# Moving work of a decoder's second layer from VectorE to ScalarE, TensorE and GpSimd

## The chip, the core and the metric

The program runs on one core of a Trainium2 chip. Five engines work beside each other and wait for one another only by semaphores: TensorE (PE, matrix products into PSUM), VectorE (DVE), ScalarE (ACT), GpSimd (POOL) and SyncE (SP, which issues transfers). The metric is the device time of one execution in microseconds (us).

## The reference

Two sequences of 512 rows by 128 columns pass through six sublayers, each followed by a layer norm of the sum with its input. The change lies in the second one (the program's "layer 2"), a cross attention with a state-space filter:

```python
Q = (x_text @ Wq).reshape(Bb, Tt, H, DH)              # Bb = 2, Tt = 512, H = 4
K = (x_vision @ Wk).reshape(Bb, Gg, H, DH)            # Gg = 77
scores = einsum('bthd,bghd->bhtg', Q, K) / sqrt(DH)   # masked by vision_mask
topv, topi = top_k(scores, 32)
attn = zeros_like(scores).at[..., topi].set(softmax(topv))
c_t = einsum('btg,bgd->btd', attn.mean(axis=1), x_vision @ Wv) * text_mask[..., None]
x = layernorm(x_text, g_norm_in, b_norm_in)
scale_in, shift_in = split(c_t @ W_film_in + b_film_in, 2)
x = x * (1.0 + mod_gate * scale_in) + mod_gate * shift_in
y = s4d(x, ...)                                       # two Fourier products and a filter
scale_out, shift_out = split(c_t @ W_film_out + b_film_out, 2)
xt = x_text + y * (1.0 + mod_gate * scale_out) + mod_gate * shift_out
h = layernorm(xt, g_ffn, b_ffn)
xt = xt + gelu(h @ W1 + b1) @ W2 + b2
return layernorm(xt, g_norm_out, b_norm_out)
```

## The kernel before, in words

The 1024 rows are eight tiles of 128 (`g` = 0 to 7), four to a sequence, which the code calls a half (`b` = 0, 1). Each engine runs a fixed list of steps, written out by hand in `first_layers`; a step is a small function, and a semaphore counts what it has done. Products land in eight PSUM banks that are handed out in a fixed order (`ring`): `claim` waits until the bank's last content was read out, `ready` and `taken` wait for it to be filled or read out.

In layer 2 each tile passes through these steps. TensorE makes its scores (`score`) and ScalarE copies them from PSUM (`scores`). VectorE takes the 32 largest of each row and head (`select`, four rounds of eight). GpSimd subtracts the maximum (`shift`), ScalarE takes the exponent (`exp`), GpSimd zeroes what was not selected (`weigh`), VectorE sums and inverts the sums and multiplies them by the text mask (`invert`), GpSimd multiplies and adds up the heads (`average`). For tiles 6 and 7 VectorE does the averages itself.

When the four averages of a half are there, TensorE turns them (`mean`), multiplies by the values (`c`, copied by ScalarE as `cT`) and by the film weights `xa_wfilm` (`film`, one product of 512 columns for each tile, in two alternating banks for half 0 and in four for half 1). VectorE reads each film bank out as film = gate * bank + `film_const`. `film_const` holds the gated bias, with 1 added to the scales, on all 128 rows; it is made early from a product of a row of ones with the bias row. For half 0 GpSimd then applies the film to `u`, the normalised input (`scale(0)`); for half 1 VectorE does. TensorE transforms `u` forth (`forth`), VectorE multiplies by the filter (`multiply`, `combine`), TensorE transforms back (`back`), VectorE adds up (`modulate`) and normalises (`norm_ff`), and the feed-forward part follows (`up`, gelu, `down`, `leave`, `move`, `finish`).

The input's normalisation is `norm_in`: VectorE takes moments, ScalarE a logarithm and an exponent for the root, VectorE refines it (`settle`) and scales four tiles (`Norm.scale`, L229). GpSimd then applies gain and bias (`affine`).

The order of the steps around the change is, on VectorE: select(2), invert(1), norm_in(0), select(3), invert(2), norm_in(1), invert(3), select(4), film(0), select(5), invert(4), select(6), invert(5), multiply(0), combine(0), select(7). On GpSimd, after weigh(3): affine(0), average(3), shift(4), weigh(4), the move of the output bias, scale(0), shift(5), average(4), skip(0), weigh(5). On TensorE: kernel, score(5), mean(0), film(0), score(6), score(7), forth(0), back(0), mean(1), film(1), up(0), size, forth(1), down(0), back(1).

Of the kernel before, what the change touches and what calls it, by code (L numbers as in the profile page):

```python
# [202 lines left out]
class Norm:  # L203
# [3 lines left out]
    def __init__(self, core):  # L207
# [11 lines left out]
        self.on_dve = self.on_act = self.shifts = self.to_apply = 0  # L219
# [16 lines left out]
    def shifts_of(self, dve, step, src, eps=1e-5):  # L236

        self.refine(dve, step, src, eps)
        k = (self.on_dve - 1) % 2
        if self.shifts:  # L240
            dve.wait_ge(self.applied, HT * self.shifts)
# [4 lines left out]
    def apply(self, act, src, dst):  # L246

        k = (self.on_act - 1) % 2
        self.to_apply += 1
        act.wait_ge(self.shift_ready, self.to_apply)  # L250
        for i in range(HT):
            act.activation(dst[:, i], src[:, i], ACT.Identity, scale=self.root[:, k, i:i + 1],  # L252
                           bias=self.shift[:, i:i + 1]).then_inc(self.applied, 1)
# [174 lines left out]
def linear_attention(core, sb, kernel, x, out):  # L428
# [36 lines left out]
    def order():  # L465
        out = [("features", 0), ("score", 0), ("features", 1)]
        for g in range(NT):
# [7 lines left out]
                   "consts": ["keys", "values", "consts"]}  # L475
# [260 lines left out]
K_TOP = 32  # L736

# [231 lines left out]
def cross_attention_ssm(core, x, x_ready, early_ring, sums_read, out):  # L969
# [27 lines left out]
    film_const = sb("xa_film_const", [P, 2, 2, P])  # L997
# [21 lines left out]
    ring.update({name: early_ring[name] for name in ("keys", "values", "consts")})  # L1019
# [13 lines left out]
    w1_ready = sem("w1_ready")  # L1033
# [19 lines left out]
    def tensor(pe):  # L1053
        def consts():
# [11 lines left out]
            pe.wait_ge(ones_ready, 1)  # L1066
            s = ring["consts"]
            s.claim(pe)
            pe.matmul(s.ps[:, :], ones[:, :], t["film_bias"][:, :], start=True, stop=True).then_inc(s.filled, 1)
# [61 lines left out]
        def film_of(b):  # L1131
# [38 lines left out]
        def up_of(b):  # L1170
# [7 lines left out]
            if b == 0:  # L1178
                pe.wait_ge(w1_ready, 1)
# [21 lines left out]
    def scalar(act, step):  # L1201
# [42 lines left out]
        def columns_of():  # L1244
            move("norm_cols", norm_cols[:, :], lambda s: s.ps[:, 0:2])
            ring["norm_cols"].taken(act)
            act.mul(w1[:, :], t["xa_w1"][:, :], norm_cols[:, 0:1]).then_inc(w1_ready, 1)
# [8 lines left out]
        def round_experts():  # L1256
# [5 lines left out]
            for n in range(4):  # L1262
# [3 lines left out]
                "taps": taps, "columns": columns_of, "kernel": kernel_of, "round": round_experts,  # L1266
                "leave": lambda b: core.norm.apply(act, xt[:, half(b)], xt[:, half(b)]),
                "finish": lambda b: core.norm.apply(act, xt[:, half(b)], out[:, half(b)])}

    def gpsimd(pool, step):  # L1270
# [67 lines left out]
    def vector(dve, step):  # L1338
        def norm_in(b):

            dve.wait_ge(x_ready, HT * (b + 1))
            core.norm.dve(dve, step, x[:, half(b)], u[:, half(b)], ready=unit_ready)
# [20 lines left out]
        def invert(g):  # L1363
# [5 lines left out]
            step(dve.tensor_reduce(total[:, k], prob[:, k], AX.X, ALU.add))  # L1369
            step(dve.reciprocal(total[:, k], total[:, k]))  # L1370
# [98 lines left out]
        def finish(b):  # L1469
            core.norm.shifts_of(dve, step, xt[:, half(b)])  # L1470
# [5 lines left out]
        def setup():  # L1476
# [3 lines left out]
            for b in range(B):  # L1480
# [9 lines left out]
            s = ring["consts"]  # L1490
            s.ready(dve)
            const = s.ps[:, :].rearrange("p (o k c) -> p o k c", o=2, k=2)
            step.mark(dve.tensor_scalar(film_const[:, :, 0], const[:, :, 0], rows["mod_gate"], 1.0, ALU.mult,
                                        ALU.add))
            dve.tensor_scalar(film_const[:, :, 1], const[:, :, 1], rows["mod_gate"], None, ALU.mult
                              ).then_inc(s.drained, 1)
            s.taken(dve)
# [2507 lines left out]
```

## Time and profile before

| | |
|---|---|
| three runs | 590.97, 595.43, 594.78 us; median 594.78 |
| profiled execution, first to last instruction | 594.2 us, mean granted TensorE clock 0.880 |
| what lies around that span | 0.58 us, if the profiled execution is taken as one at the median |
| PE busy | 478.3 us (80%) |
| DVE busy | 431.7 us (73%) |
| ACT busy | 273.4 us (46%) |
| POOL busy | 248.9 us (42%) |

The shares are means over six sublayers with different limits, so they say little of one stage. The second layer runs from about 84 to 201 us of the span.

### The profile page before, as it was taken

How to read it: one execution, taken by the hardware profiler on the slowest of the kernel's cores; microseconds unless marked ns; L12 is line 12 of the kernel's file. 1: busy time of each engine (PE TensorE's matmuls, PEld its weight loads, DVE VectorE, ACT ScalarE, POOL GpSimd, SP SyncE). 2: the span in 40 equal slices, each digit the busy share in tenths (PEclk: the TensorE clock that was granted, in tenths of full speed). 3: DMA queues.
4: the chain of work that ended last, by engine and by line, in shares of the span. 5: the costliest groups of instructions: out<-in, count | busy, mean ns of one | idle time of the engine just before them, and what ended most of it. 6: DMA issues, size and time to landing. Idle time of an engine off the chain costs nothing. (4 is left out here: it accounts for less than half of the span.)

```text
span 594.2 us, 11914 instructions
## 1 busy us (share of the span) xinstructions
PE 478.3 (80%) x4082; PEld 361.4 (61%) x4082; DVE 431.7 (73%) x1456; ACT 273.4 (46%) x681; POOL 248.9 (42%) x295
## 2 busy tenths in 40 slices
PE   3888782779679685799898999887779879779994
PEld 1455442555648664777694668765358755369983
DVE  4687968797986846855687999996487748327743
ACT  4599570221213245355412768552335413547741
POOL 3631399456812102455201524340485333616650
PEclk9986895587789877799999999979878989969997
DMA  8300004410000005605200000000471500151113
GB/s 253 109 2 1 1 2 144 122 57 2 1 1 1 1 1 141 142 2 105 40 1 1 2 2 2 1 2 3 165 318 30 121 0 26 52 151 47 46 48 104
DMA packets 27998, 33.37 MB, mean 56 GB/s; under 512 B 4962, under 2 KB 21074, under 8 KB 27427
## 3 DMA queue, kind: packets, MB, share of 16 engines
q1 hardware_dynamic: 26002, 29.13, 16.8%
q0 software_dynamic: 1504, 3.15, 1.6%
q8 instruction: 34, 0.56, 0.4%
q10 hardware_dynamic: 432, 0.33, 0.2%
q14 instruction: 26, 0.21, 0.1%
HBM read 26.44 MB, written 6.16 MB: 55 GB/s over the span
## 5 line engine op out<-in xcount | busy, mean ns | idle before, releaser
L2133 POOL TENSOR_TENSOR ea_scaled_rows<-ea_scaled_rows 128x768 f32<-128x768 f32 (+2 forms) x21 | 24.0, 1142 | 50.7 <-ACT ea_scaled_rows L2047 49.6
L3725 POOL DMA_INDIRECT em_results<-em_y_slot,slot_rows x31 | 29.7, 958 | 28.7 <-DVE em_y_slot L3852 28.1
L288 ACT ACTIVATE norm_log<-norm_var 128x4 f32<-128x4 f32 x20 | 4.1, 205 | 73.6 <-DVE norm_var L269 73.6
L3584 PE MATMUL banks<-em_slotT,em_weights 128*128 128x128 f32 x248 | 35.0, 287 | 2.6 <-ACT em_weights L3473 2.6
L3843 DVE SCALAR_TENSOR_TENSOR em_innerT<-banks,em_bias_of,em_soft 128x128 f32<-128x128 f32 x62 | 18.9, 347 | 23.0 <-ACT em_soft L3667 20.2
L38 PE MATMUL banks<-ea_w_high,ea_x_high 128*128 128x384 f32 x64 | 27.2, 425 | 8.7 <-DVE ea_acc L2224 8.5
L3584 PEld LDWEIGHTS banks<-em_slotT,em_weights 128*128 128x128 f32 x248 | 32.1, 202 | 3.3 <-issue 3.3
L2047 ACT ACTIVATE ea_scaled_rows<-banks,ea_gate 128x192 f32<-128x192 f32 x64 | 23.3, 418 | 18.8 <-PE banks L38 18.6
L2795 POOL TENSOR_TENSOR ga_to_end<-ga_cum 128x512 f32<-128x512 f32 x8 | 9.1, 1137 | 45.0 <-DVE ga_to_mid L2857 45.0
L3667 ACT ACTIVATE em_soft<-banks,em_bias_of 128x128 f32<-128x128 f32 x62 | 19.4, 364 | 12.3 <-PE banks L3584 11.7
L38 PE MATMUL banks<-ea_w_high,ea_x_low 128*128 128x384 f32 x64 | 23.7, 371 | 0.0
L38 PE MATMUL banks<-ea_w_low,ea_x_high 128*128 128x384 f32 x64 | 23.7, 370 | 0.0
L3241 POOL TENSOR_TENSOR ca_prob<-ca_prob,ca_most 128x1232 f32<-128x1232 f32 x8 | 18.0, 2250 | 11.1 <-DVE ca_most L3293 11.1
L648 POOL TENSOR_TENSOR lin_q_strip<-lin_qT,lin_strip_head 128x512 f32<-128x512 f32 x8 | 9.5, 1199 | 29.6 <-PE banks L538 20.3
L3720 POOL DMA_INDIRECT em_slots<-em_sent,em_where x16 | 15.7, 981 | 14.2 <-DVE em_where L3794 9.6
L2220 DVE SCALAR_TENSOR_TENSOR ea_acc<-banks,ea_gate,ea_acc 128x192 f32<-128x192 f32 x24 | 10.0, 418 | 15.8 <-PE banks L38 15.5
L38 PEld LDWEIGHTS banks<-ea_w_high,ea_x_high 128*128 128x128 f32 x64 | 13.7, 214 | 11.0 <-DVE ea_acc L2224 9.6
L1356 DVE MATCH_REPLACE8 xa_left<-xa_top,xa_left 128x77 f32<-128x77 f32 x96 | 20.3, 225 | 0.0
L3596 PE MATMUL banks<-em_down,em_innerT 128*128 x124 | 18.9, 276 | 0.6 <-DVE em_innerT L3843 0.6
L538 PE MATMUL banks<-lin_q_strip,lin_kT 32*128 32x512 f32 x64 | 12.1, 832 | 8.8 <-DVE lin_scores L682 8.3
L3183 ACT ACTIVATE ca_prob<-ca_prob 128x1232 f32<-128x1232 f32 x8 | 9.8, 1231 | 19.7 <-POOL ca_prob L3241 19.7
L682 DVE TENSOR_TENSOR lin_scores<-banks,causal 128x2048 f32<-128x2048 f32 x8 | 18.2, 2272 | 0.0
(522 smaller groups left out, 1539.4 us busy)
## 6 DMA issues: line engine op xcount, KB each, us to landing
em_up<-in_em_up SPq DMA_DIRECT2D x3, 1536.0 KB, 10.8
ea_wide<-ea_gates SPq DMA_DIRECT2D x4, 1024.0 KB, 11.7
em_down<-in_em_down SPq DMA_DIRECT2D x3, 768.0 KB, 12.2
em_slots<-slot_rows SPq DMA_DIRECT2D x1, 2108.0 KB, 10.8
w_qkv<-in_w_qkv SPq DMA_DIRECT2D x1, 1536.0 KB, 7.4
slot_rows<-em_slots SPq DMA_DIRECT2D x1, 1360.0 KB, 8.5
cos_half<-in_cos_half SPq DMA_DIRECT2D x1, 1024.0 KB, 7.1
sin_half<-in_sin_half SPq DMA_DIRECT2D x1, 1024.0 KB, 9.3
```

The source lines that it names most:

```text
L38: ins = pe.matmul(out, weights[w], data[d], start=(start and n == 0), stop=(stop and n == 2), **kw)
L682: dve.tensor_tensor(scores[:, g % 2].rearrange("p r j t -> p (r j) t"), scored.rearrange("p r j t -> p (r j) t"), spread(causal[:, :], 1, ...
L1356: ins = dve.match_replace(left[:, k, hh], top[:, k, r, hh], src[:, k, hh], SELECTED)
L2047: ins = act.activation(scaled_rows[:, g % 2, j - 1 + n], s.ps[:, n * QKV:(n + 1) * QKV], ACT.Copy, scale=gate[:, g, e:e + 1])
L2133: step(pool.tensor_tensor(scaled_rows[:, k, 0:n], scaled_rows[:, k, 0:n], scaled_rows[:, k, n:2 * n], ALU.add))
L3241: pool.tensor_tensor(p, p, spread(most[:, g % AHEAD], 2, [P, H, G]), ALU.subtract).then_inc(shifted, 1)
L3584: ins = pe.matmul(s.ps[:, k * P:(k + 1) * P], weights[:, n % NW, k // 2, k % 2 * P:(k % 2 + 1) * P], slotT[:, n], start=True, stop=True, s ...
L3596: ins = pe.matmul(s.ps[:, 0:P], innerT[:, n % NW, j], down_all[:, bass.ds(e, 1), j, :], start=(j == 0), stop=(j == 1))
L3667: act.activation(soft[:, n % NW, j], s.ps[:, j * P:(j + 1) * P], ACT.Silu, bias=bias_of[:, j, n:n + 1]).then_inc(soft_ready, 1)
L3720: pool.indirect_dma_start(core.slots[:, :], bass.IndirectOffsetOnAxis(ap=where[:, k, i:i + 1], axis=0), sent[:, i, k, :], None).then_inc(c ...
L3725: pool.indirect_dma_start(core.results[:, :], bass.IndirectOffsetOnAxis(ap=slot_rows[:, s, P:P + 1].bitcast(U32), axis=0), y_slot[:, s % N ...
L3843: dve.scalar_tensor_tensor(innerT[:, n % NW, j], s.ps[:, HE + j * P:HE + (j + 1) * P], bias_of[:, 2 + j, n:n + 1], soft[:, n % NW, j], ALU ...
```

## The change

It has four parts, all in layer 2.

1. The gate and the bias of the film move into the product. ScalarE multiplies `xa_wfilm` by the gate once (`film_weight`). VectorE gates the bias row, one partition, in place of the constants on 128. In `film_of` TensorE makes two products for each tile: ones times the bias row, then `cT` times the weights, added in the same bank. The early product for `film_const` and its bank go.
2. Film half 0 leaves PSUM by four ScalarE copies, after exp(4). VectorE's film(0) step goes; film(1) stays with VectorE and becomes a plain copy.
3. The input normalisation's scalings go to ScalarE. VectorE makes a row of shifts (`shifts_of`), and ScalarE applies root and shift to four tiles in one activation each (`enter`), behind film_weight and the root in its list, ahead of exp(2) for half 0 and of the filter's copies for half 1.
4. For tiles 0 to 5 the text mask is applied by GpSimd, as a first operation of `average`.

```diff
-                   "consts": ["keys", "values", "consts"]}
+                   "consts": ["keys", "values"]}
...
-            pe.wait_ge(ones_ready, 1)
-            s = ring["consts"]
-            s.claim(pe)
-            pe.matmul(s.ps[:, :], ones[:, :], t["film_bias"][:, :], start=True, stop=True).then_inc(s.filled, 1)
...
-            s.taken(pe)
+            if b == 0:
+                pe.wait_ge(consts_ready, 3)
+                pe.wait_ge(weights_ready, 2)
             for g in range(HT * b, HT * b + HT):
                 s = ring[f"film{g}"]
                 s.claim(pe)
-                pe.matmul(s.ps[:, :], cT[:, g], t["xa_wfilm"][:, :], start=True, stop=True).then_inc(s.filled, 1)
+                pe.matmul(s.ps[:, :], ones[:, :], t["film_bias"][:, :], start=True, stop=False)
+                if g == HT * b:
+                    ring[f"c{b}"].taken(pe)
+                pe.matmul(s.ps[:, :], cT[:, g], t["xa_wfilm"][:, :], start=False, stop=True).then_inc(s.filled, 1)
...
+        def film_weight():
+            core.wait_loaded(act, "xa")
+            act.mul(t["xa_wfilm"][:, :], t["xa_wfilm"][:, :], rows["mod_gate"]).then_inc(weights_ready, 1)
+
+        def film_of(b):
+            for g in range(HT * b, HT * b + HT):
+                move(f"film{g}", film[:, g].rearrange("p k c -> p (k c)"))
...
+                "enter": lambda b: core.norm.apply(act, x[:, half(b)], u[:, half(b)], unit_ready),
...
             pool.wait_ge(total_ready, g + 1)
+            step(pool.tensor_scalar(total[:, k], total[:, k], text_weight[:, g:g + 1], None, ALU.mult))
...
-            core.norm.dve(dve, step, x[:, half(b)], u[:, half(b)], ready=unit_ready)
+            core.norm.shifts_of(dve, step, x[:, half(b)], after=(unit_ready, HT * b) if b else None)
...
+            if g < LAST_AVERAGES:
+                dve.reciprocal(total[:, k], total[:, k]).then_inc(total_ready, 1)
+                return
...
-                dve.scalar_tensor_tensor(film[:, g].rearrange("p k c -> p (k c)"), s.ps[:, :],
-                                         rows["mod_gate"],
-                                         film_const[:, :, :, :].rearrange("p o k c -> p (o k c)"),
-                                         ALU.mult, ALU.add).then_inc(s.drained, 1)
+                dve.tensor_copy(film[:, g].rearrange("p k c -> p (k c)"), s.ps[:, :]).then_inc(s.drained, 1)
...
+            two["film_weight"]()
             core.norm.act(act, step)
+            two["enter"](0)
             two["exp"](2)
...
             core.norm.act(act, step)
+            two["enter"](1)
             two["kernel"]()
...
             two["exp"](4)
+            two["film"](0)
             two["scores"](6)
...
-            two["film"](0)
             two["select"](5)
```

On TensorE, mean(0) to forth(0) stood in this order (`xa_mean` are the averages, `xa_k_wide` and `xa_mask_row` belong to score):

```order
L1128 MATMUL banks<-ident,xa_mean 77x128 x4
L1136 MATMUL banks<-xa_meanT,xa_v 128x512
L1141 MATMUL banks<-xa_wfilm,xa_cT 128x512 x4
L1092 MATMUL banks<-xa_k_wide,xa_qT 128x308
L1093 MATMUL banks<-xa_mask_row,xa_ones 128x308
```

Of the changed kernel the same place, on the same engine, reads so (the pair of film rows stands four times):

```order
L1131 MATMUL banks<-ident,xa_mean 77x128 x4
L1139 MATMUL banks<-xa_meanT,xa_v 128x512
L1146 MATMUL banks<-film_bias,xa_ones 128x512
L1149 MATMUL banks<-xa_wfilm,xa_cT 128x512
L1095 MATMUL banks<-xa_k_wide,xa_qT 128x308
L1096 MATMUL banks<-xa_mask_row,xa_ones 128x308
```

Four products became eight between `c` and the scores of tile 6; mean(1) and film(1), ahead of up(0), changed in the same way.

On VectorE, the second normalisation to select(5) stood so before (of select's rounds the first stands here):

```order
L277 SCALAR_TENSOR_TENSOR norm_root<-norm_square,norm_root 128x4
L229 TENSOR_SCALAR xa_u<-x,norm_mean_var,norm_root 128x128 x4
L1369 TENSOR_REDUCE xa_total<-xa_prob 128x4
L1370 RECIPROCAL xa_total<-xa_total 128x4
L1371 TENSOR_SCALAR xa_total<-xa_total,xa_text_weight 128x4
L1353 MAX xa_top<-xa_score 128x8 x4
...
L1393 SCALAR_TENSOR_TENSOR xa_film<-banks,rows,xa_film_const 128x512 x4
```

In the changed kernel VectorE has there:

```order
L283 SCALAR_TENSOR_TENSOR norm_root<-norm_square,norm_root 128x4
L245 SCALAR_TENSOR_TENSOR norm_shift<-norm_mean_var,norm_root 128x4
L1388 TENSOR_REDUCE xa_total<-xa_prob 128x4
L1390 RECIPROCAL xa_total<-xa_total 128x4
L1372 MAX xa_top<-xa_score 128x8 x4
L1375 MATCH_REPLACE xa_left<-xa_top,xa_score 128x77 x4
```

The four scalings became one small row of shifts, the mask's multiplication left, and select(5) now follows select(4) with no film between them.

## Rows read from the trace of the kernel before

**Rows 1.** Busy time by stretch: us, PE, PEld, DVE, ACT, POOL, PEclk, DMA share, GB/s

```profile
84.00:169.00 85.00, 56.82 (x510) 42.29 (x510) 74.68 (x475) 16.65 (x44) 57.09 (x65) 0.72 0.18 57
169.00:201.00 32.00, 29.21 (x185) 22.59 (x185) 24.93 (x68) 8.02 (x16) 4.25 (x3) 0.95 0.01 1
```

**Rows 2.** Timeline of DVE: start, us, instructions, [idle before them <- releaser]

```profile
114.20 1.12 DVE L229 TENSOR_SCALAR xa_u<-x,norm_mean_var,norm_root 128x128 f32<-128x128 f32 x4
124.30 3.34 DVE L229 TENSOR_SCALAR xa_u<-x,norm_mean_var,norm_root 128x128 f32<-128x128 f32 x4
128.27 0.23 DVE L1371 TENSOR_SCALAR xa_total<-xa_total,xa_text_weight 128x4 f32<-128x4 f32 x1
136.23 0.75 DVE L1393 SCALAR_TENSOR_TENSOR xa_film<-banks,rows,xa_film_const 128x512 f32<-128x512 f32 x1 [2.17 <-PE banks L1141]
139.75 0.75 DVE L1393 SCALAR_TENSOR_TENSOR xa_film<-banks,rows,xa_film_const 128x512 f32<-128x512 f32 x1 [0.36 <-PE banks L1141]
152.86 0.47 DVE L1369 TENSOR_REDUCE xa_total<-xa_prob 128x4 f32<-128x308 f32 x1 [0.38 <-issue]
193.28 0.69 DVE L1452 TENSOR_TENSOR xa_xt<-banks,xa_u 128x512 f32<-128x512 f32 x1 [0.38 <-PE banks L1193]
```

**Rows 3.** Timeline of POOL, from affine(0) to weigh(5)

```profile
126.47 1.09 POOL L1275 TENSOR_TENSOR xa_u<-xa_u,rows 128x512 f32<-128x512 f32 x1
128.58 0.70 POOL L1298 TENSOR_TENSOR xa_prob<-xa_prob,xa_total 128x308 f32<-128x308 f32 x1 [1.02 <-DVE xa_total L1371]
129.89 0.31 POOL L1300 TENSOR_TENSOR xa_mean<-xa_prob 128x77 f32<-128x77 f32 x1
...
146.14 0.70 POOL L1284 TENSOR_TENSOR xa_prob<-xa_score,xa_top 128x308 f32<-128x308 f32 x1 [2.78 <-DVE xa_left L1356]
...
150.87 0.98 POOL L1291 TENSOR_SCALAR xa_left<-xa_left 128x308 f32<-128x308 f32 x1
151.94 0.84 POOL L1292 TENSOR_TENSOR xa_prob<-xa_left,xa_prob 128x308 f32<-128x308 f32 x1
```

**Rows 4.** Timeline of PE, half 0: mean(0), c, film(0), forth(0)

```profile
130.26 0.33 PE L1128 MATMUL banks<-ident,xa_mean 128*77 128x128 f32 x1 [2.85 <-POOL xa_mean L1300]
131.31 2.05 PE L1136 MATMUL banks<-xa_meanT,xa_v 77*128 77x512 f32 x2 [0.72 <-issue]
134.03 5.68 PE L1141 MATMUL banks<-xa_wfilm,xa_cT 128*128 128x512 f32 x8 [0.68 <-ACT xa_cT L1205]
...
143.46 5.44 PE L1152 MATMUL banks<-xa_u,cos_half 128*128 128x128 f32 x32 [1.09 <-issue]
148.74 3.74 PE L1152 MATMUL banks<-xa_u,sin_half 128*128 128x128 f32 x32
```

**Rows 5.** Timeline of PE, half 1: mean(1), c, film(1), up(0)

```profile
168.96 0.33 PE L1128 MATMUL banks<-ident,xa_mean 128*77 128x128 f32 x1 [1.72 <-DVE xa_mean L1387]
170.01 1.10 PE L1136 MATMUL banks<-xa_meanT,xa_v 77*128 77x512 f32 x2 [0.72 <-issue]
171.78 5.32 PE L1141 MATMUL banks<-xa_wfilm,xa_cT 128*128 128x512 f32 x8 [0.67 <-ACT xa_cT L1205]
176.94 0.60 PE L1175 MATMUL banks<-ident,xa_h 128*128 128x128 f32 x4
```

**Rows 6.** Timeline of PE, the early product of ones and bias row

```profile
30.61 1.09 PE L1069 MATMUL banks<-film_bias,xa_ones 1*128 1x512 f32 x2 [1.57 <-DVE lin_yT L702]
```

**Rows 7.** Timeline of ACT: the scaling of another weight by a column

```profile
107.02 0.72 ACT L1247 ACTIVATE xa_w_scaled<-xa_w,xa_norm_cols 128x512 f32<-128x512 f32 x1
```

**Rows 8.** Root and shift applied by ACT elsewhere: ns min/median/max, first and last start

```profile
L252 ACT ACTIVATE x<-xa_xt,norm_shift,norm_root x8: 477/478/493, 202.0 to 232.5; 128x128 f32<-128x128 f32 x8
```

**Rows 9.** Stretches of 2 us, columns as in rows 1: the clock in film(0), film(1)

```profile
132.00:134.00 2.00, 1.36 (x2) 0.00 (x0) 2.00 (x19) 0.59 (x1) 0.00 (x0) 0.50 0.00 0
136.00:138.00 2.00, 2.00 (x4) 0.72 (x3) 0.97 (x2) 0.00 (x0) 1.92 (x3) 0.62 0.01 4
172.00:174.00 2.00, 2.00 (x3) 0.96 (x4) 1.35 (x10) 0.41 (x2) 0.00 (x0) 0.50 0.00 0
```

More of the change, by code:

```diff
@@ L218, in __init__ @@
         self.shift_ready, self.applied = core.sem("shift_ready"), core.sem("norm_applied")
-        self.on_dve = self.on_act = self.shifts = self.to_apply = 0
+        self.on_dve = self.on_act = self.shifts = self.to_apply = self.elsewhere = 0
     def dve(self, dve, step, src, dst, eps=1e-5, ready=None):
@@ L234, in scale, with shifts_of @@
                 ins.then_inc(ready, 1)
-    def shifts_of(self, dve, step, src, eps=1e-5):
+    def shifts_of(self, dve, step, src, eps=1e-5, after=None):
         self.refine(dve, step, src, eps)
         k = (self.on_dve - 1) % 2
-        if self.shifts:
-            dve.wait_ge(self.applied, HT * self.shifts)
+        if after is not None:
+            dve.wait_ge(*after)
+        elif self.shifts > self.elsewhere:
+            dve.wait_ge(self.applied, HT * (self.shifts - self.elsewhere))
         self.shifts += 1
@@ L244, in shifts_of, with apply @@
                                  ).then_inc(self.shift_ready, 1)
-    def apply(self, act, src, dst):
+    def apply(self, act, src, dst, done=None):
         k = (self.on_act - 1) % 2
+        if done is None:
+            done = self.applied
+        else:
+            self.elsewhere += 1
         self.to_apply += 1
@@ L252, in apply @@
             act.activation(dst[:, i], src[:, i], ACT.Identity, scale=self.root[:, k, i:i + 1],
-                           bias=self.shift[:, i:i + 1]).then_inc(self.applied, 1)
+                           bias=self.shift[:, i:i + 1]).then_inc(done, 1)
     def refine(self, dve, step, src, eps):
@@ L736 @@
 K_TOP = 32
+LAST_AVERAGES = NT - 2
 class StateSpaceKernel:
@@ L996, in cross_attention_ssm @@
     u = sb("xa_u", [P, NT, P])
-    film_const = sb("xa_film_const", [P, 2, 2, P])
+    sb("xa_room_ahead", [P, 4, P])
     norm_cols = sb("xa_norm_cols", [P, 2])
@@ L1018, in cross_attention_ssm @@
     ring.update(core.ring.plan([f"s{g}" for g in range(HT, NT)], (0, 1, 2, 5)))
-    ring.update({name: early_ring[name] for name in ("keys", "values", "consts")})
+    ring.update({name: early_ring[name] for name in ("keys", "values")})
     work = {b: {"mean": [f"meanT{b}"], "film": [f"c{b}"] + [f"film{g}" for g in range(HT * b, HT * b + HT)],
@@ L1032, in cross_attention_ssm @@
     weighed, total_ready = sem("weighed"), sem("total_ready")
-    w1_ready = sem("w1_ready")
+    weights_ready = sem("weights_ready")
     unit_ready, normed = sem("unit_ready"), sem("normed")
@@ L1178, in up_of @@
             if b == 0:
-                pe.wait_ge(w1_ready, 1)
+                pe.wait_ge(weights_ready, 1)
             for j in range(4):
@@ L1246, in columns_of @@
             ring["norm_cols"].taken(act)
-            act.mul(w1[:, :], t["xa_w1"][:, :], norm_cols[:, 0:1]).then_inc(w1_ready, 1)
+            act.mul(w1[:, :], t["xa_w1"][:, :], norm_cols[:, 0:1]).then_inc(weights_ready, 1)
+        def film_weight():
[4 more added lines that the diff above has]
+                move(f"film{g}", film[:, g].rearrange("p k c -> p (k c)"))
         def kernel_of():
@@ L1266, in scalar @@
                 "taps": taps, "columns": columns_of, "kernel": kernel_of, "round": round_experts,
+                "film_weight": film_weight, "film": film_of,
+                "enter": lambda b: core.norm.apply(act, x[:, half(b)], u[:, half(b)], unit_ready),
                 "leave": lambda b: core.norm.apply(act, xt[:, half(b)], xt[:, half(b)]),
@@ L1469, in finish @@
         def finish(b):
-            core.norm.shifts_of(dve, step, xt[:, half(b)])
+            core.norm.shifts_of(dve, step, xt[:, half(b)], after=None if b else (unit_ready, B * HT))
             var, root = core.norm.last()
@@ L1489, in setup @@
             step.mark(dve.memset(total[:, :, :], 0.0))
[L1490 to L1497, printed above, removed]
+            row = t["film_bias"][:, :].rearrange("p (o k c) -> p o k c", o=2, k=2)
+            gate = rows["mod_gate"][0:1]
+            step.mark(dve.tensor_scalar(row[:, :, 0], row[:, :, 0], gate, 1.0, ALU.mult, ALU.add))
+            dve.tensor_scalar(row[:, :, 1], row[:, :, 1], gate, None, ALU.mult).then_inc(consts_ready, 1)
+            dve.wait_ge(consts_ready, 3)
             step.wait()
@@ L1679, in _ @@
                     two["shift"](g + 1)
-                if g < NT - 2:
+                if g < LAST_AVERAGES:
                     two["average"](g)
@@ L1816, in expert_attention @@
     prob, probT = sb("ea_prob", [P, 2, HT * P]), sb("ea_probT", [P, 2, HT, P])
-    sb = hole("xa_film_const", "kernel_im")
+    sb = hole("xa_room_ahead", "kernel_im")
     attT, res = (sb(f"ea_{n}", [P, NT, P]) for n in ("attT", "res"))
@@ L3490, in _ @@
                     if b == 0:
-                        sp.wait_ge(core.norm.applied, HT * (core.norm.to_apply + 1))
+                        sp.wait_ge(core.norm.applied, HT * (core.norm.to_apply - core.norm.elsewhere + 1))
                     else:
```

## The prediction

> **What bounds the kernel now.** I read the busy times by stretch first, then the timelines of VectorE, GpSimd and TensorE through layer 2, then what each gap waits for. Layer 2 has two parts with different limits. From 84 to 169 us VectorE is busy 74.68 of 85 us and nobody else is near that; from 169 to 201 us TensorE is busy 29.21 of 32 [rows 1]. The reader should see that the change relieves VectorE in both parts, and loads TensorE in both.
>
> In the first part VectorE's list is long, but some of its time is waiting. It stands at film(0): it starts waiting at 134.06 (136.23 less 2.17) and is through at 140.50, 6.4 us for four bank reads of 0.75 [rows 2]. The scalings of norm_in(1) take 3.34 us against 1.12 in norm_in(0) [rows 2]; what stretched them these rows don't say, but VectorE gets all of it back. Both times vanish from its list. In the second part the chain is TensorE's alone: mean(1), c, film(1), then up(0) in the same moment (176.94) [rows 5], and so on to down(0), for which VectorE's leave(0) waits the last 0.38 us [rows 2]. A microsecond more in film(1) is a microsecond more at leave(0), and everything behind leave(0) hangs on it.
>
> **Early part.** The removed product took 1.09 us and TensorE had waited 1.57 us ahead of it [rows 6]; two small VectorE operations change with it. Between 0 and -1.1 us; I take 0, since the product stood in a place where TensorE was ahead of VectorE.
>
> **Half 0, the start.** The last average of half 0, average(3), starts on GpSimd at 128.58 after waiting 1.02 us for invert(3) on VectorE [rows 3]. invert(3) stood behind the 3.34 us of scalings; without them, and without four mask multiplications of 0.23 [rows 2], it is done before affine(0) ends at 127.56 (126.47 + 1.09), so the wait goes. affine(0) itself comes about 0.3 earlier, because the scaling of norm_in(0) leaves VectorE too (about 0.9 net of a small row of shifts), less some 0.6 for film_weight, which stands ahead of that norm's root on ScalarE and costs about what its like does, 0.72 [rows 7]. ScalarE's eight scalings at 0.48 [rows 8] lie in its idle time: it is busy 16.65 of 85 us [rows 1]. Against this, average(3) gets a mask operation on GpSimd: between 0 and 0.98 (the same operation on 308 columns); the row of 77 columns took 0.31 [rows 3] and is nearest, so 0.3. Sum: mean(0)'s last turn moves from 130.26 to about 129.2, 1.05 us earlier, and c from 131.31 to 130.25 [rows 4].
>
> The Trainium skill, GPSIMD Engine Reference, section 3.1, puts an elementwise operation on GpSimd at about twice VectorE's time; that would make 0.46 of the 0.23, and c would start 0.15 later.
>
> **Half 0, film(0).** A product of 512 columns costs 1.09 us from a row of ones [rows 6] and 1.10 from 77 rows [rows 5] at full clock, and 2.05 [rows 4] where the granted clock is 0.50 [rows 9], that is 1.2 instead of 2.4 GHz. So the row products are as dear as the real ones. Before, the clock had fallen by the time of c, and came back inside film(0) between 136 and 138 us [rows 9], after some 4 us in which TensorE had worked without a pause since 134.03; film(0) ended at 139.7 (134.03 + 5.68) [rows 4]. After, c starts at 130.25 and straddles the fall, 1.3 us; the first row product fills the wait for cT (0.68 in rows 4). So the engine works without a pause from 130.25, and I put the return of the clock at about 134.5. Row product 131.55 to 133.65 at 2.1; the first film product across the return, to 135.05; six more at 1.08: 141.5. film(0) thus ends 1.8 us later, though it started earlier.
>
> **Half 0, behind it.** ScalarE's copies (about 0.6, as other moves of a bank) instead of 0.75: the last film is out at 142.1 against 140.5. scale(0) takes 2.6 us, to 144.8 against 143.36. Before, GpSimd then waited 2.78 us, to 146.14, for select(5) on VectorE [rows 3], which stood behind film(0); now select(5) is done near 137, so shift(5) starts at 144.8, 1.3 earlier. With 0.3 for average(4)'s mask, weigh(5) ends at 151.7 instead of 152.78 (151.94 + 0.84) [rows 3], and invert(5) follows there, not at 152.86 [rows 2]. multiply(0) also needs forth(0). It started at 143.46 and took 9.0 us, the first half 5.44 partly at the low clock, the second 3.74 [rows 4]. It now starts at 144.9, but the scores of tiles 6 and 7 come directly ahead of it, TensorE doesn't pause, and I take 2 x 3.74: it ends at 152.4, as before (152.48). invert(5), freed of its own mask operation (0.23), is done 1.4 us earlier, and multiply(0), two operations of about 0.6 on each half of forth(0), finds the second half ready. So select(7), and with it average(7), starts 1.4 us earlier. That is all that is left of some 10 us of VectorE time: VectorE stands idle instead, about 6 us ahead of select(6), whose scores now come behind film(0) on both TensorE and ScalarE.
>
> **Half 1.** mean(1)'s last turn moves from 168.96 to 167.55 and c from 170.01 to 168.6. At full clock c and eight products take 1.1 + 8 x 1.08 = 9.7, to 178.3; the first row product covers the wait for cT (0.67), the others are in the open. Before, film(1) took 5.32 instead of 4.3, as the clock was 0.50 from 172 on [rows 9], after the same pause ahead of mean(1) (1.72) [rows 5]. That pause stays, so I leave a low stretch. It cost 1.0 before; now the first row product stands where the wait was, and if c and that product run low they lose 0.95 and 1.0. Between 0 and 1.95 I take 1.6, nearer to the upper end since the pause is the same: film(1) ends at 179.9, and up(0) starts there instead of at 176.94. VectorE's copies of film(1) and scale(1) need some 2.2 us after that, hT, up(0) and size on TensorE over 5, so forth(1) doesn't wait for them. **Sum:** -1.4 us to mean(1), +4.4 from there to up(0) (12.35 us from 167.55 to 179.9 against 7.98 from 168.96 to 176.94), together +3.0, and nothing on the chain from there to leave(0) gives it back: span 594.2 + 3.0 = 597.2, and 594.8 + 3.0 = 597.8 for the median (which I take 0.6 above the span, as what lies around it).
>
> **Rivals.** *A: the clock holds.* The longer unbroken runs keep TensorE at 2.4 GHz through both films. c from 130.25 takes 1.1, the row product hides in the wait, seven more at 1.08 end at 139.9, 0.2 after the old end; GpSimd ends scale(0) at 143.3 as before and, free of its 2.78 but for the mask's 0.3, weigh(5) at 150.3; forth(0) ends at 150.9, select(7) starts 2.9 earlier, and film(1) ends at 168.96 - 2.9 + 1.05 + 9.7 = 176.8, 0.1 earlier than before: 594.7. For it: film(0) rises in its midst as soon as the engine doesn't pause; against it: the pauses ahead of mean(0) (2.85) and mean(1) (1.72) stand before the products, not between them. The Trainium skill, TensorE: Matmul & The Clock Gate, "What's actually happening", says the same in general, that lower clock is the rest state and activity lifts it; by that rule the change helps itself, and A is its case. The rows agree that it rises during film(0).
>
> *B: the clock comes back no sooner.* In film(0) it returns at 137.9 as before: ends 143.2, forth(0) starts at 146.5 and takes its old 9.0; it ends at 155.5, select(7) is 0.5 later than before, c starts at 170.5 and takes 2.05, one product 2.1, one across the return 1.4, six 1.08: film(1) ends at 182.5, 5.6 late: 600.4.
>
> *C, the other side: row products don't bring the clock back.* If the engine, fed by one row in every second product, stays at 1.2 GHz, each film takes 8 x 2.1 = 16.8. film(0) ends at 148.3 (131.55 + 16.8), forth(0) starts at 151.6 and ends at 160.6, 8.1 late, of which VectorE had 2.5 to spare: select(7) starts 5.6 late, and film(1) ends at 168.96 + 5.6 + 1.05 + 2.05 + 16.8 = 194.5 against 176.94: +17.5, 612.3. It decides as soon as a film shows no rise at all. Against it: no row shows a low clock through so long a busy run.
>
> *D: TensorE isn't the limit of the second part.* If norm_ff(0) on VectorE set up(0), the extra products would be covered and 1.4 us gained: 593.4. Against it: up(0) starts at 176.94 with film(1)'s end and no idle noted [rows 5].
>
> **Numbers.** Forecast 0.50, A 0.20, B 0.17, C 0.06, D 0.04; 0.03 for something that moves by over 1% downwards unseen. About 1%, here 5.9 us, is what a measurement can tell from no change. The range goes from A less the spread of the three runs to either side (2 us), 592.5, to B with somewhat under that, 602. Faster by over 1% (below 588.9): 0.03. Slower by over 1% (above 600.7): C, and 0.06 of B with the spread: 0.12. Within: 0.85.
>
> **What would show it.** Right: in the new trace VectorE waits some 6 us for ScalarE's copy ahead of select(6); shift(5) on GpSimd waits for nothing; film(1) takes 8.6 to 10.6 us and up(0) begins with its end; forth(0) runs at one clock. A: granted clock 1.00 through both films. B and C: 0.50 in most of them. Wrong: a wait on VectorE behind enter(0) or enter(1) (exp(2) and exp(3) stand behind these on ScalarE, and weigh(2) and weigh(3) on GpSimd wait for them), a mask operation on GpSimd near 1 us, which would put 0.7 on each average, or forth(0) waiting for GpSimd beyond 146.5.

## The result, and the profile after

| | before | after |
|---|---|---|
| median | 594.78 us | 610.75 us (608.96 to 613.67, 5 runs) |
| ratio to the kernel before | | 1.0332, 95% interval 1.0286 to 1.0378 |
| span of the profiled execution | 594.2 us | 607.2 us |
| mean granted TensorE clock | 0.880 | 0.856 |
| PE busy | 478.3 us | 503.0 us |
| DVE busy | 431.7 us | 421.0 us |

The kernel is 3.3% slower: 16.0 us by the medians, where 3.0 were forecast. It is outside the range, and close to rival C (612.3). VectorE was relieved as meant, by 10.7 us; TensorE works 24.7 us longer. Ratios, here and below, leave disturbed runs out and medians don't, which is why the two don't always agree.

Busy time by stretch of the changed kernel (columns as in rows 1), the two large stretches first, then stretches of 2 us:

```profile
84.00:169.00 85.00, 65.41 (x495) 43.29 (x495) 62.05 (x443) 21.37 (x52) 55.99 (x69) 0.64 0.17 57
169.00:201.00 32.00, 29.88 (x106) 15.16 (x105) 18.04 (x42) 7.58 (x12) 4.24 (x3) 0.73 0.00 1
...
132.00:134.00 2.00, 2.00 (x3) 0.50 (x2) 2.00 (x19) 0.58 (x1) 2.00 (x3) 0.50 0.00 0
...
142.00:144.00 2.00, 2.00 (x3) 0.50 (x2) 0.00 (x0) 0.00 (x0) 0.00 (x0) 0.50 0.00 0
...
146.00:148.00 2.00, 2.00 (x7) 0.88 (x6) 0.51 (x4) 0.41 (x1) 1.83 (x2) 0.97 0.00 0
...
182.00:184.00 2.00, 2.00 (x3) 0.50 (x4) 0.15 (x1) 0.00 (x0) 0.00 (x0) 0.50 0.00 0
...
192.00:194.00 2.00, 2.00 (x4) 0.89 (x3) 2.00 (x3) 1.99 (x3) 2.00 (x2) 0.52 0.00 0
194.00:196.00 2.00, 2.00 (x11) 1.28 (x11) 0.93 (x1) 1.40 (x3) 0.51 (x1) 1.00 0.00 0
```

In the second stretch the clock is 0.73 instead of 0.95 [rows 1]. The reader should look at PE and PEclk of one row together: from 132 to 144 us TensorE is busy in 2.00 of every 2.00 us, and the clock stays at 0.50. Before, it came back between 136 and 138 us [rows 9].

Timeline of PE of the changed kernel, both films:

```profile
127.04 0.33 PE L1131 MATMUL banks<-ident,xa_mean 128*77 128x128 f32 x1 [1.87 <-POOL xa_mean L1319]
128.09 1.10 PE L1139 MATMUL banks<-xa_meanT,xa_v 77*128 77x512 f32 x2 [0.72 <-issue]
129.12 2.07 PE L1146 MATMUL banks<-film_bias,xa_ones 1*128 1x512 f32 x2
131.12 2.08 PE L1149 MATMUL banks<-xa_wfilm,xa_cT 128*128 128x512 f32 x2
...
143.14 2.08 PE L1149 MATMUL banks<-xa_wfilm,xa_cT 128*128 128x512 f32 x2
...
148.79 5.44 PE L1160 MATMUL banks<-xa_u,cos_half 128*128 128x128 f32 x32 [0.41 <-issue]
154.06 3.74 PE L1160 MATMUL banks<-xa_u,sin_half 128*128 128x128 f32 x32
...
172.09 0.33 PE L1131 MATMUL banks<-ident,xa_mean 128*77 128x128 f32 x1 [0.73 <-DVE xa_mean L1409]
...
174.16 1.12 PE L1146 MATMUL banks<-film_bias,xa_ones 1*128 1x512 f32 x2
175.22 1.13 PE L1149 MATMUL banks<-xa_wfilm,xa_cT 128*128 128x512 f32 x2
176.27 1.53 PE L1146 MATMUL banks<-film_bias,xa_ones 1*128 1x512 f32 x2
177.73 2.08 PE L1149 MATMUL banks<-xa_wfilm,xa_cT 128*128 128x512 f32 x2
...
187.61 1.06 PE L1183 MATMUL banks<-ident,xa_h 128*128 128x128 f32 x4
189.35 5.96 PE L1191 MATMUL banks<-xa_hT,xa_w_scaled 128*128 128x512 f32 x8 [0.68 <-ACT xa_hT L1213]
```

Eight products of film(0), each 2.07 or 2.08 us, follow one another without a gap from 129.12 to 145.2; before, it was 5.68 us for all [rows 4]. Film(1) starts at full clock and drops in its third product; the other five don't get it back, and it returns only at about 194 us, near the end of up(0) (5.96 us, before 3.70).

Timeline of VectorE of the changed kernel: select(6), a copy of film(1), leave(0).

```profile
147.49 0.66 DVE L1372 MAX8 xa_top<-xa_score 128x8 f32<-128x77 f32 x4 [12.30 <-ACT xa_score L1213]
...
183.85 0.69 DVE L1415 COPY xa_film<-banks 128x512 f32<-128x512 f32 x1 [3.31 <-PE banks L1149]
...
206.28 0.69 DVE L1471 TENSOR_TENSOR xa_xt<-banks,xa_u 128x512 f32<-128x512 f32 x1 [0.38 <-PE banks L1201]
```

Timeline of GpSimd there: average(3) with the mask, scale(0), shift(5).

```profile
124.98 0.30 POOL L1316 TENSOR_SCALAR xa_total<-xa_total,xa_text_weight 128x4 f32<-128x4 f32 x1
125.36 0.70 POOL L1317 TENSOR_TENSOR xa_prob<-xa_prob,xa_total 128x308 f32<-128x308 f32 x1
...
146.09 1.26 POOL L1326 TENSOR_TENSOR xa_u<-xa_u,xa_film 128x512 f32<-128x512 f32 x1 [11.70 <-ACT xa_film L1213]
147.43 1.26 POOL L1327 TENSOR_TENSOR xa_u<-xa_u,xa_film 128x512 f32<-128x512 f32 x1
148.65 0.70 POOL L1302 TENSOR_TENSOR xa_prob<-xa_score,xa_top 128x308 f32<-128x308 f32 x1
```

Timeline of ScalarE there: film_weight, the last copy of film(0), finish(0).

```profile
110.72 0.72 ACT L1259 ACTIVATE xa_wfilm<-xa_wfilm,rows 128x512 f32<-128x512 f32 x1
...
145.25 0.58 ACT L1213 COPY xa_film<-banks 128x512 f32<-128x512 f32 x1 [3.42 <-PE banks L1149]
...
214.99 1.65 ACT L258 ACTIVATE x<-xa_xt,norm_shift,norm_root 128x128 f32<-128x128 f32 x4 [0.82 <-DVE norm_shift L245]
```

All three stand and wait for TensorE: VectorE 12.30 us ahead of select(6), GpSimd 11.70 ahead of scale(0), ScalarE 3.42 ahead of a copy. leave(0) on VectorE comes at 206.28 instead of 193.28 [rows 2], 13.0 later, which is the difference of the spans. That this is less than the medians' 16.0 lies in which executions were profiled: layer 1 was 2.8 us quicker in this one (GpSimd's `near` waves start at 65.63 against 68.40). It isn't the edit, since a kernel below that shares none of it has 65.79 there (the kernel before with unread products of 128 rows). What lies around the span is 1.8 us (608.96 against 607.2), not the 0.58 that the table ahead of the prediction took; the forecast was added to the median, so this doesn't change it.

To compare executions whose layer 1 differs, I count from the start of mean(0)'s last turn, by three marks: mean(1)'s last turn, up(0) (its first transpose), and finish(0) on ScalarE (the row at 214.99 above; 201.99 before). In microseconds, each from the mark ahead of it:

| kernel | mean(0) at | to mean(1) | to up(0) | to finish(0) | sum |
|---|---|---|---|---|---|
| before | 130.26 | 38.70 | 7.98 | 25.05 | 71.73 |
| after | 127.04 | 45.05 | 15.52 | 27.38 | 87.95 |

So the change costs 16.2 us here: 6.4 by film(0), 7.5 by film(1), and 2.3 because up(0) runs at 1.2 GHz. The experiments below have the same line. The span's rest behind finish(0) varies between 389 and 400 us over the twelve kernels, though the steps there are the same, so that the sums show better than a single span what an edit does in layer 2. But they are read from one execution of each kernel; that the rest doesn't depend on the edit is not shown.

### The profile page after: what moved, and what is told of

The parts are those of the page before. It is cut to its first block and busy times, and to the rows that moved or that the text cites. A ratio compares the mean times of both kernels' runs of the same rounds, so it can differ in the third digit from the quotient of the medians.

```text
span 607.2 us, 11945 instructions
## 1 busy us (share of the span) xinstructions
PE 503.0 (83%) x4096; PEld 370.2 (61%) x4096; DVE 421.0 (69%) x1440; ACT 279.6 (46%) x694; POOL 253.5 (42%) x301
## 3 DMA queue, kind: packets, MB, share of 16 engines
q1 hardware_dynamic: 26002, 29.13, 16.2%
## 5 line engine op out<-in xcount | busy, mean ns | idle before, releaser
L38 PE MATMUL banks<-ea_w_high,ea_x_high 128*128 128x384 f32 x64 | 27.4, 428 | 8.6 <-DVE ea_acc L2243 8.5
L654 POOL TENSOR_TENSOR lin_q_strip<-lin_qT,lin_strip_head 128x512 f32<-128x512 f32 x8 | 12.1, 1517 | 23.9 <-PE banks L544 14.6
```

The lines of the kernel that those rows point to most:

```text
L38: ins = pe.matmul(out, weights[w], data[d], start=(start and n == 0), stop=(stop and n == 2), **kw)
```

## The experiments

Theory 1: products of one row hold TensorE, but the clock doesn't come back while they stand among the film's products. Rivals: theory 2, it is the number of products on the path; theory 3, it is two products added up in one bank. The first four kernels tell these apart.

**No one-row products.**

```diff
-                pe.matmul(s.ps[:, :], ones[:, :], t["film_bias"][:, :], start=True, stop=False)
-                pe.matmul(s.ps[:, :], cT[:, g], t["xa_wfilm"][:, :], start=False, stop=True).then_inc(s.filled, 1)
+                pe.matmul(s.ps[:, :], cT[:, g], t["xa_wfilm"][:, :], start=True, stop=True).then_inc(s.filled, 1)
```

> The changed kernel without its eight one-row products: each film bank gets the film product alone, and the bias of the film is left out of what is computed. Theory 1 (one-row products hold TensorE and don't bring its clock back): film(0) runs as in the kernel before, 5.3 to 6 us after the copy of c, film(1) 5.3 us with up(0) at full clock (3.7 us), and the kernel takes 590 to 594 us. Theory 2 (eight products more on the path, of whatever kind, and the clock low by chance of timing) expects the same here. Should the rest of the change (norm scaling on ScalarE, mask on GpSimd) be what costs the time, it stays at 605 us or more.

Measured: 590.53 us, 0.9858 (0.9814 to 0.9901). This is inside theory 1's 590 to 594 us, which theory 2 expected too: the loss is all in these eight products, and the rest of the change is a gain. Timeline of PE:

```profile
129.92 6.57 PE L1148 MATMUL banks<-xa_wfilm,xa_cT 128*128 128x512 f32 x8 [0.77 <-ACT xa_cT L1212]
...
165.83 5.37 PE L1148 MATMUL banks<-xa_wfilm,xa_cT 128*128 128x512 f32 x8 [0.77 <-ACT xa_cT L1212]
...
172.31 3.70 PE L1190 MATMUL banks<-xa_hT,xa_w_scaled 128*128 128x512 f32 x8 [0.68 <-ACT xa_hT L1212]
```

**The bias product on 128 rows.**

```diff
-                pe.matmul(s.ps[:, :], ones[:, :], t["film_bias"][:, :], start=True, stop=False)
+                pe.matmul(s.ps[:, :], share, t["film_bias"][:, :], start=True, stop=False)
...
-            gate = rows["mod_gate"][0:1]
+            gate = rows["mod_gate"]
...
+            dve.memset(share, 1.0 / P)
```

`share` is a 128x128 tile, and `film_bias` is loaded into 128 partitions.

> The changed kernel with the bias products made on 128 rows: weights 1/128 in a 128x128 tile, the gated bias loaded into 128 partitions, so the same 512 columns, the same sums, the same two products in one bank. Theory 1: the granted clock comes back inside film(0), at about 134 to 138 us, half 1 has no more than a short low stretch (film(1) 8.6 to 10.6 us, up(0) 3.7 us) and the kernel takes 596 to 600 us. Theory 2: the same as the change, 608 to 613 us. Theory 3 (a second product into one bank is what is slow): also 608 to 613 us.

Measured: 593.18 us, 0.994 (0.991 to 0.997), 0.6% under the kernel before and some 3 us better than theory 1's range. The same number of products, of the same 512 columns, into the same banks, one pair after the other: theories 2 and 3 fall. Stretches of this kernel (columns as in rows 1), then the PE timeline of film(0) and up(0):

```profile
128.00:130.00 2.00, 2.00 (x4) 0.67 (x2) 2.00 (x18) 0.63 (x2) 0.70 (x1) 0.53 0.02 4
130.00:132.00 2.00, 2.00 (x4) 0.83 (x3) 2.00 (x19) 0.31 (x1) 1.51 (x2) 0.62 0.00 0
132.00:134.00 2.00, 2.00 (x6) 0.95 (x5) 2.00 (x19) 0.63 (x2) 2.00 (x3) 1.00 0.00 0
```

```profile
129.13 1.91 PE L1148 MATMUL banks<-film_bias,xa_room_ahead 128*128 128x512 f32 x2
130.84 1.37 PE L1151 MATMUL banks<-xa_wfilm,xa_cT 128*128 128x512 f32 x2
132.04 1.02 PE L1148 MATMUL banks<-film_bias,xa_room_ahead 128*128 128x512 f32 x2
...
174.47 3.70 PE L1193 MATMUL banks<-xa_hT,xa_w_scaled 128*128 128x512 f32 x8 [0.68 <-ACT xa_hT L1215]
```

The clock falls at about 128 us and is back within the first pair, in its film product (1.37 us; from the second pair on a product takes 1.02). With one row it fell at about 129 us and came back at about 146. In half 1 it doesn't fall at all. At full clock a product starts every 0.86 us here (132.04, 132.90), where with one-row products in turn it was 1.05 (174.16, 175.22, 176.27 above); so film(1)'s eight products take 7.1 us, less than the 8.6 that I expected at the least, which is part of what puts the time under the range.

**Unread products in the kernel before**, once of one row, once of 128, each ahead of a film product and overwritten by it (the wait for cT comes behind the first of them, as in the change):

```diff
+                unread(pe, s, ones[:, :], t["film_bias"][:, :], 1)
```

```diff
+                unread(pe, s, ident[:, :], t["xa_wfilm"][:, :], 1)
```

> The kernel before with one unread one-row product (ones by the film bias) ahead of each of its eight film products, into the same bank, each product starting the bank anew; everything else as before. Theory 1: 607 to 613 us, film(0) and film(1) at 2.07 us a product and up(0) at 6 us. Theory 2: the same, 607 to 613 us. Theory 3 (two products added up in one bank): 596 to 600 us.

> As the run with unread one-row products, but each unread product is of 128 rows (the identity by the film weight, 512 columns). Theory 1: the clock comes back during film(0) and stays in half 1, 596 to 601 us. Theory 2: 607 to 613 us, as with one row. Theory 3: 596 to 601 us.

Measured: one row 618.04 us, 1.0264 (1.0172 to 1.0356; four runs from 608.5 to 620.7); 128 rows 600.19 us, 1.0087 (1.0038 to 1.0135). The kernel before had 596.52 us in that round, so the first ratio stands for about 612 us, inside theory 1's 607 to 613, while the median of the four lies above it; the second is in the range of theories 1 and 3. Since nothing is added up in a bank here and no other part of the change is in these kernels, one-row products are enough by themselves; what eight products cost as such is the 128-row kernel's 0.9%. In the one-row kernel film(0)'s products take 2.07 us each from 133.09 to 149.0, and film(1)'s from its third on. Timelines of PE in film(0), first with one row, then with 128:

```profile
133.09 2.07 PE L364 MATMUL banks<-film_bias,xa_ones 1*128 1x512 f32 x2
135.09 2.07 PE L1143 MATMUL banks<-xa_wfilm,xa_cT 128*128 128x512 f32 x2
```

```profile
130.88 1.02 PE L364 MATMUL banks<-xa_wfilm,ident 128*128 128x512 f32 x2
131.74 1.02 PE L1143 MATMUL banks<-xa_wfilm,xa_cT 128*128 128x512 f32 x2
```

The one-row execution was the longest of its four (620.71 us), so that its sum in the next table is rather too high.

**One row in half 0, 128 rows in half 1.**

```diff
+                pe.matmul(s.ps[:, :], share if b else ones[:, :], t["film_bias"][:, :] if b else t["film_bias"][0:1, :],
+                          start=True, stop=False)
```

> The changed kernel with the bias product of half 0 on one row and that of half 1 on 128 rows (weights 1/128). Theory 1: the clock falls in half 0's film and stays low to 145 us as in the change, which moves select(7) by some 3 us, and half 1 (film(1) in 7 to 9 us, up(0) in 3.7 us) is as with 128 rows: 597 to 602 us. Theory 2: as the change, 608 to 613 us.

Measured: 608.46 us, 1.0214 (1.0141 to 1.0287): above theory 1's range, at the lower end of theory 2's. But the kernel before had 597.50 us in this round instead of 594.78; by the ratios it lies below the change's 1.0332, its interval ending where that one's begins (1.0287 and 1.0286). The marks, with the kernels to compare it with:

| kernel | mean(0) at | to mean(1) | to up(0) | to finish(0) | sum |
|---|---|---|---|---|---|
| 128 rows in both halves | 126.64 | 37.62 | 8.94 | 25.05 | 71.61 |
| one row in half 0 | 130.16 | 45.54 | 10.55 | 25.05 | 81.14 |
| one row in both (after) | 127.04 | 45.05 | 15.52 | 27.38 | 87.95 |
| no bias product | 126.96 | 35.96 | 8.12 | 25.05 | 69.13 |
| one row, unread, in the kernel before | 130.06 | 48.38 | 16.76 | 27.78 | 92.92 |
| 128 rows, unread, in the kernel before | 125.49 | 39.95 | 10.55 | 25.05 | 75.55 |

Half 1 went as theory 1 says (10.55, up(0) at full clock). I had priced half 0 too low: 3 us for select(7)'s delay, where it is 6.8 us against the kernel before (45.54 to 38.70) and 7.9 against 128 rows in both halves.

**Half 1's one-row products first, then its four film products.**

```diff
+            if b:
+                for g in range(HT, NT):
+                    bias_row(g)
```

`bias_row` claims the bank and makes the one-row product.

> The changed kernel with half 1's four one-row products issued first, one to each of the four banks, and then its four film products in a row; half 0 as in the change, the same instructions in all. Theory 1 with the film's own products bringing the clock back once no one-row product stands between them: film(1) ends 1 to 3 us earlier than in the change and up(0) runs in 3.7 to 4.8 us, 604 to 608 us. If the order makes no difference to the clock: 609 to 613 us.

Measured: 618.11 us, 1.0369 (1.0293 to 1.0444): outside both ranges, though by the ratios not told apart from the change (1.0332). In half 1 up(0) did what theory 1 says; film(1) didn't end earlier. Timeline of PE:

```profile
177.70 2.05 PE L1139 MATMUL banks<-xa_meanT,xa_v 77*128 77x512 f32 x2 [0.72 <-issue]
179.68 7.19 PE L1146 MATMUL banks<-film_bias,xa_ones 1*128 1x512 f32 x8
186.80 5.91 PE L1156 MATMUL banks<-xa_wfilm,xa_cT 128*128 128x512 f32 x8
192.55 0.60 PE L1190 MATMUL banks<-ident,xa_h 128*128 128x128 f32 x4
193.82 3.70 PE L1198 MATMUL banks<-xa_hT,xa_w_scaled 128*128 128x512 f32 x8 [0.68 <-ACT xa_hT L1220]
```

Four film products in a row take 5.91 us, so the clock rises within them, and up(0) has its 3.70 again: 25.05 to finish(0). But c already ran at 1.2 GHz here, so that up(0) starts 15.90 us behind mean(1) against 15.52 in the change. Half 0, whose code is that of the change, took 47.90 us to mean(1) instead of 45.05: sum 88.85. Its trace shows where: c ran at 1.2 GHz there too (2.00 us against 1.10), and the clock stayed at 0.50 through the scores of tiles 6 and 7, in which a one-row product of the mask follows each of 128 rows, and into forth(0), to about 157 us. In the change it was back at about 146, in the first of those products. Why it came back later these runs don't settle.

**The film as before, parts 3 and 4 of the change kept** (the norm's scalings on ScalarE, the mask on GpSimd). VectorE's list has film(0) behind select(4) again.

```diff
-                dve.tensor_copy(film[:, g].rearrange("p k c -> p (k c)"), s.ps[:, :]).then_inc(s.drained, 1)
+                dve.scalar_tensor_tensor(film[:, g].rearrange("p k c -> p (k c)"), s.ps[:, :],
+                                         rows["mod_gate"],
+                                         film_const[:, :, :, :].rearrange("p o k c -> p (o k c)"),
+                                         ALU.mult, ALU.add).then_inc(s.drained, 1)
```

> The changed kernel with the film put back as it was (VectorE takes both halves out of the banks with gate and constant in one operation, no one-row products at the film): of the change only the input normalisation's scalings on ScalarE and the mask on GpSimd are left. Theory 1 (the loss is the one-row products and the clock alone; these two parts are worth the 1.0 us that average(3) waited, or a little more): 0.99 to 1.00 of the kernel before, some 1 to 4 us less. Rival (they cost something of their own, by affine's later start or the mask operation on GpSimd): 1 us or more above the kernel before.

Measured: 590.82 us, 0.9894 (0.9829 to 0.996), at the lower edge of theory 1's range and against the rival. Its profile shows little of that gain: from the start of GpSimd's `near` waves to mean(0)'s last turn it is 61.32 us against 61.86, and 72.02 from there to finish(0) against 71.73. Where the rest comes from stays open.

**Gate, bias and values put together early.** If the bias must be a row, it can be a row of a product that is made anyway, away from the path. The values times the gated film weight are made once for each half, with the bias as row 0; the film is then one product for each tile from the turned means, and c is left out.

```diff
+                pe.matmul(s.ps[0:G + 1, :], v[:, b], t["xa_wfilm"][:, :], start=True, stop=False)
+                pe.matmul(s.ps[0:G + 1, :], ident[0:1, 0:G + 1], t["film_bias"][:, :], start=False,
+                          stop=True).then_inc(s.filled, 1)
...
-                pe.matmul(s.ps[:, :], cT[:, g], t["xa_wfilm"][:, :], start=False, stop=True).then_inc(s.filled, 1)
+                pe.matmul(s.ps[:, :], meanT[:, g], wide[:, b], start=True, stop=True).then_inc(s.filled, 1)
```

> A version with the bias and the value product put together early: the values times the gated film weight, with the gated bias as one more row, are made once for each half on TensorE (two products of 128 rows and two of one row, at about 100 us) and kept; the film is then one product for each tile from the turned means with 78 rows, and the product c with its copy is left out. ScalarE takes half 0's film as in the change. Theory 1: with no one-row products at the film the clock behaves as in the kernel before; saved on the path are c with its copy, 2.7 us in half 0 and 1.8 us in half 1, beside what the change without row products saved (0.986 of the kernel before): 0.975 to 0.987, 581 to 588 us. Rival: products of 78 rows don't bring the clock back either, and film(0) at 2.07 us each leaves it at 0.99 to 1.00.

Then the same made earlier, and that with the means filled up with zeros from 78 columns to 128:

```diff
                 two["score"](g)
+            two["wide"]()
             two["taps"]()
```

> As the version that makes the gated, biased film weight for each half early, but made still earlier, ahead of the taps, where TensorE waited 11 us for GpSimd (87 to 98 us in its trace); there its four products took 7.7 us at 115.7 to 123.4 us, at 1.2 GHz, ahead of the kernel's products. Film products of 78 rows as there. Expected of theory 1: mean(0)'s last turn at 128 to 131 us instead of 134, 582 to 588 us, 0.975 to 0.988 of the kernel before. If half 1's film of 78 rows leaves the clock at 0.50 through up(0), as it did there (169 to 179 us), up(0) takes some 6 us again.

```diff
-    means = sb("xa_mean", [P, NT, G + 1])
+    means = sb("xa_mean", [P, NT, P])
```

> The same with the means filled up to 128 columns and the weight to 128 rows with zeros, so that the film products have 128 rows, 50 of them zeros; the same sums. If the rows of a product are what counts for the clock, even rows of zeros, it is back within half 1's film (about 4 us after its start) and up(0) takes 3.7 to 4.5 us: 1 to 3 us less than with 78 rows. If rows of zeros don't count, half 1 is as with 78 rows (up(0) some 6 us), the same time within 1 us.

Measured: made ahead of the filter's products 590.06 us, 0.9911 (0.9874 to 0.9947); made ahead of the taps 592.56 us, 1.0001 (0.9966 to 1.0035); that with zeros to 128 rows 586.65 us, **0.9877** (0.9801 to 0.9954), the fastest median of all kernels here. By the ratios it isn't told apart from the kernel without the bias product (0.9858) or from the film as before with parts 3 and 4 kept (0.9894). The first two missed their ranges; the first came out at its rival's 0.99 to 1.00, but not in the rival's way, since its film(0) of 78 rows ran at full clock (3.79 us). The third gained 5.9 us on the second, where 1 to 3 were expected. In the first, the early products ran at 1.2 GHz from 115.74 to 123.4 us and pushed mean(0) to 133.97, and up(0) took 6.47 us; with that place put right in the second, mean(0)'s last turn came at 127.38, and the clock was low in both films. The third shows what the rows do to it. Timelines of PE, film(0), film(1) and up(0), first with 78 rows, then with 128 (both made ahead of the taps):

```profile
128.36 7.20 PE L1150 MATMUL banks<-xa_wide,xa_meanT 78*128 78x512 f32 x8 [0.67 <-ACT xa_meanT L1214]
...
164.64 6.69 PE L1150 MATMUL banks<-xa_wide,xa_meanT 78*128 78x512 f32 x8 [0.67 <-ACT xa_meanT L1214]
...
172.85 6.66 PE L1192 MATMUL banks<-xa_hT,xa_w_scaled 128*128 128x512 f32 x8 [0.68 <-ACT xa_hT L1214]
```

```profile
126.95 5.61 PE L1149 MATMUL banks<-xa_wide,xa_meanT 128*128 128x512 f32 x8 [0.68 <-ACT xa_meanT L1213]
...
159.99 3.70 PE L1149 MATMUL banks<-xa_wide,xa_meanT 128*128 128x512 f32 x8 [0.67 <-ACT xa_meanT L1213]
...
166.11 3.70 PE L1191 MATMUL banks<-xa_hT,xa_w_scaled 128*128 128x512 f32 x8 [0.68 <-ACT xa_hT L1213]
```

Stretches of the two, again first with 78 rows:

```profile
130.00:132.00 2.00, 2.00 (x4) 0.68 (x3) 2.00 (x19) 0.93 (x2) 1.34 (x3) 0.50 0.01 4
```

```profile
130.00:132.00 2.00, 2.00 (x4) 0.79 (x5) 2.00 (x19) 0.56 (x2) 1.92 (x3) 0.63 0.00 0
```

In half 0 the clock fell at about 128 us in both. With 128 rows, 50 of them zeros, it was back between 130 and 132 us; with 78 rows it was at 0.50 to the end of film(0) at 135.4 and on, through the scores and most of forth(0)'s first half, until 144. The sums are 63.94 (33.04, 5.79, 25.11) with 128 rows and 71.81 (36.28, 7.46, 28.07) with 78. Half 1 alone would not decide it, since in the 128-row kernel the clock hadn't fallen there at all; that rows of zeros count as rows rests on this one stretch of one execution.

## Why the prediction was wrong

**The step that failed** is the return of the clock in film(0): "the engine works without a pause from 130.25, and I put the return of the clock at about 134.5". It took working without a pause as what brought the clock back before. In the two films that I had seen those were products of 128 rows, and I carried it over to products of one row, of which the rows only showed how long they take. In the changed kernel the engine works without a pause from 128.09 on, and the clock is at 0.50 from about 129 to 146 us: film(0) takes 16.1 us where the forecast has 10.0 (131.55 to 141.5). With 128 rows in place of one, and the products otherwise the same, it is back within some 4 us of its fall.

The Trainium skill, TensorE: Matmul & The Clock Gate, "What's actually happening", has the clock rise with how busy TensorE has been. These runs don't bear that out if busy means occupied: from 132 to 144 us TensorE is busy 2.00 of every 2.00 us, at 0.50.

**Half 1** failed at the same step: I left one low stretch that cost 1.6 us; it was the five last products and most of up(0). The term was +4.4 from mean(1) to up(0); measured are 7.5, and 2.3 more behind up(0)'s start, which no case of mine had.

**Rival C** was this case, at 0.06. Its film(0) takes 16.8 us, measured 16.1; from mean(0) to mean(1) it makes 6.65 us more (5.6 and the 1.05 by which mean(0) comes earlier), measured 6.4; its film(1), all at half clock, was too dear (it starts at full clock), and it lacks the 2.3 of up(0); 612.3 against 610.75. What I set against it, "no row shows a low clock through so long a busy run", was true and no evidence: no row showed so long a run with one-row products in it either. The trace of the kernel before has a short one, the scores of tiles 6 and 7, from 139.55 to 142.37 us: in those 2.8 us the clock stayed at 1.00, but it was there already.

**Right were** the price of a one-row product (1.12 us at full clock, 2.07 at half); average(3)'s wait gone and GpSimd's mask operation 0.30 us; film_weight 0.72; shift(5) without a wait behind scale(0) (148.65), though 3.9 us later than I said; VectorE idle ahead of select(6), 12.30 us where I had 6; up(0) beginning with film(1)'s end; leave(0) carrying the sum to the end unchanged. Of the early gain of 1.05 at mean(0) about 0.45 was found, counted from GpSimd's `near` waves (61.41 us against 61.86). The Trainium skill's factor of two for GpSimd (GPSIMD Engine Reference, section 3.1), cited beside that term, would have made the mask operation 0.46; the row says 0.30.

**forth(0)** was to run at one clock, 2 x 3.74; it took 5.44 and 3.74, as before. The pause ahead of it had shrunk from 1.09 to 0.41 us, and the clock fell in forth(0) all the same; why is not shown.

## What to carry to other kernels

Price a product on TensorE by its time and, apart from that, by what it does to the clock of the products around it: here eight bias products cost 18.8 us by the marks as one row (87.95 against 69.13) and 2.5 us on 128 rows (71.61), each read from one execution. A rise of the clock that a trace shows holds for the kind of products that it shows it with; carry it over to another kind only after a run. A row that must be added to a product can go into one that is made once and away from the path, and if that leaves fewer than 128 rows, filling them with zeros was worth 5.9 us here (592.56 to 586.65). It is no clear gain over leaving the bias with VectorE, where the copy out of the bank adds it (0.9877 and 0.9894).

## What I hadn't expected of the hardware

- One-row products in turn with products of 128 rows, TensorE without a gap: 0.50 for 16 us and more, in half 0 of all four kernels that had them there (129 to 146 us in the change), and in half 1 of the change from about 177 to 194 us, of which up(0)'s products of 128 rows hold the last 4.6.
- Film products of 78 rows, made ahead of the taps: the clock stayed at 0.50 from about 128 to 144 us, 7 us of it film products, and in half 1 through film(1) and most of up(0)'s products of 128 rows until about 179 us. With 50 rows of zeros more it returned within some 4 us of its fall in half 0.
- up(0) to finish(0) took 25.05 us in seven kernels whose up(0) ran at full clock (25.11 in one more), and 27.4 to 28.1 in four whose up(0) didn't.
